# A graph kernel: low parts of the value items, taken from a ScalarE copy and subtracted later

## The chip, the cores and the metric

The kernel runs on one core of a Trainium2 chip. The metric is the device time of one execution in microseconds (us). PE is TensorE, DVE is VectorE, ACT is ScalarE, POOL is GpSimd, SP is SyncE; PEld is TensorE's loading of weights.

## The reference, cut to what matters

1024 nodes with 512 features, 16384 edges (src, dst) sorted by dst.

```
h = relu(layernorm(x));  q, k, v = h @ Wq + bq, h @ Wk + bk, h @ Wv + bv
adj[src, dst] = 1
a = where(adj, q @ k.T / sqrt(512), -1e6)
x = x + softmax(a) @ v
h = relu(layernorm(x))
deg = number of edges into a node + 1;  w = deg^-0.5[src] * deg^-0.5[dst]   # with self loops
agg(y) = segment_sum(w * y[dst], src)
x = x + agg(relu(batchnorm(agg(h @ W1 + b1))) @ W2 + b2)
```

What the change touches is `h @ Wv`, 1024x512, and `softmax(a) @ v`.

## The kernel before, in words

**Products in parts.** Most operands are held as two parts of TensorE's rounded format (fp32r): high = the rounded value, low = the value minus high. A product is three matmuls (lines 955 to 957): low x high, high x low, high x high. So every product that is used again is evacuated from PSUM twice: ScalarE writes the high part (hi_of, line 450), VectorE subtracts it from the same PSUM bank to give the low part (lo_of, line 645).

**Items.** A piece of such work is called an item: "t" (a transposed weight), "m" (Wq Wk^T), "h" (128 rows of h, transposed), "v" (128 rows of h @ Wv, eight of them), "q" (128 columns for 512 rows of the query side), "w" (a row for the mask level). `items` lists them in TensorE's order, and `nth(item)` is an item's place in it, counted from 1. The semaphores item_ps (TensorE done), item_hi (ScalarE done) and item_lo (VectorE done) count in this order. TensorE's make(item) (line 971) waits until the last item in the same PSUM bank has its low part (`last_in`, line 183), and an item that reads others waits for their low parts by item_lo.

**Counting stage.** The adjacency counts are made in 16 windows of 64 target nodes (window 0, 1, ... in the order of work). The edges of a window come in chunks of 128. For each block of two or three chunks VectorE writes one-hot matrices, src_oh (line 674) and dst_oh (line 676), into a ring of four slots; TensorE multiplies them (line 1021), and a last matmul closes the window (line 1035). VectorE may write a slot again when TensorE has used it. ScalarE evicts the counts (counts, line 446), two banks taking turns. In between, items are worked off: before window i TensorE and ScalarE take the items `ahead[i]`, and VectorE takes their low parts two windows later, before its one-hots of window i + 2:

```
for i in range(2, NW):
    for item in ahead[i - 2]:
        lo_of(item)
    ...
    onehots(i, now)
```

The value items are in `ahead[2]` (v0, v1), `ahead[3]`, `ahead[4]` (v2, v3, each with an h item) and `ahead[6]` to `ahead[9]` (v4 to v7); `ahead[5]` holds two h items, `ahead[10]` to `ahead[13]` the first four q items, `ahead[15]` the w item.

**After the counts.** VectorE computes the mask level, the degrees (line 759) and the low part of the item q(1, 0) (line 763). GpSimd computes deg^-0.5 and then adds the value bias to four tiles of x (add_bv, line 381). TensorE goes over eight row tiles: scores(t) (line 1068), with the q items of the second half between the first ones, then weighted_v(t) (line 1082), the product of the probabilities p with all value items, and later products. For a tile VectorE masks the scores (line 775) and takes the maximum, ScalarE takes exp and writes the high part of p in half precision, VectorE its low part (line 787), two DMAs transpose the parts, and ScalarE (line 515) and VectorE (line 797) bring them back into p's place for weighted_v. Behind the first masking VectorE also finds whether a count is too large (large_flag, line 765). The order on each engine is that of the code.

**Places.** `v` is [128, 8, 2, 512] in fp32r: per value item its high part, then its low part.

Of the kernel before, what the change touches and what calls it, by code (L numbers as in the profile page):

```python
# [17 lines left out]
P = 128  # L18
N = 1024
D = 512  # L20
# [36 lines left out]
def gnn_kernel(nc, x, src, dst, Wq, bq, Wk, bk, Wv, bv, W1, b1, gamma, beta, W2, b2, out):  # L57
# [14 lines left out]
    def hold(name, kib):  # L72
# [18 lines left out]
        [("pT_place2", [P, 2, 2, NT, P], F32R), ("w2_raw", [P, 2, KC, D], F32)],  # L91
        [("g32", [P, KC, N], F32)])
    hold("region_WT", 32)
    v, zT, edge_i, edge_f, chunk1, hit, reach = shared(
        [("v", [P, NT, 2, D], F32R)], [("zT", [P, 2, KC, N], F32R)],
        [("edge_i", [P, 2, P], I32), ("edge_f", [P, 2, P], F32), ("chunk1", [P, 2, NCH], F32),
         ("hit", [P, 2, NCH], F32), ("reach", [P, 2, NCH], F32)])
    hold("region_v", 32)
# [57 lines left out]
    dst_in src_in ext_ready ext_ps edge_f_ready ecol_ps ecol_ready drel_ready lim_ready lim_ps bounds_ready  # L156
    x_in0 x_in1 x_in2 x_in3 qk_bias_in bcol_in bias_in b1_in
    Wk_in0 Wk_in1 Wq_in0 Wq_in1 wB_in0 wB_in1 w2_in0 w2_in1 w_hi w_lo
    x_sums x_means x_squares ln_scale ln_coef h_ready item_ps item_hi item_lo uw_ready hw_second fill_ready
    onehots onehots_used c_done c16 loops_added adj_in0 adj_in1 adj_in2 adj_in3  # L160
    deg_ready degm_ready degm_ps flag_ready dinv_ready
    s_ps mask_set masked top_ready exp_done rinv_ready p16_hi p16_lo p16_hi_in p16_lo_in p_hi p_lo pv_ps xb_ready x1_ready
# [16 lines left out]
    final = {("q", 1, c): 4 + c for c in range(KC)}  # L179
    items = list(start) + sum(ahead, []) + list(final)  # L180
    nth = lambda item: items.index(item) + 1
    item_bank = lambda item: start.get(item, final.get(item, 2 + (items.index(item) - len(start)) % ITEM_BANKS))
    last_in = lambda b, end: max([n for n, other in enumerate(items[:end], 1) if item_bank(other) == b] + [0])

    drel = lambda i: (drel_first if i < NW // 2 else drel_second)[:, i % (NW // 2), :]
    row_of = lambda t: T[:, t // 2, t % 2 * D:(t % 2 + 1) * D] if t < KC else hrow[:, t - KC, :]
# [222 lines left out]
    def _(act):  # L409
# [40 lines left out]
        def hi_of(item):  # L450

            what, n, c = item
            act.wait_ge(S["item_ps"], nth(item))
            if what == "q":
                if item == ("q", 0, 0):
                    act.wait_ge(S["uw_ready"], 4)
                if item == ("q", 1, 0):
                    act.wait_ge(S["c_done"], NW)
                act.activation(item_dest(item, 0), item_ps(item), ACT.Identity,
                               bias=uw[:, 0, c:c + 1]).then_inc(S["item_hi"], 1)  # L460
            else:
                act.activation(item_dest(item, 0), item_ps(item), ACT.Copy).then_inc(S["item_hi"], 1)

        def mask_fill(t):

# [131 lines left out]
    def _(dve):  # L597
# [47 lines left out]
        def lo_of(item):  # L645

            what, n, c = item
            dve.wait_ge(S["item_hi"], nth(item))
            hi = item_dest(item, 0).bitcast(F32)
            if what == "w":  # L650
                times_w_row(range(KC)).then_inc(S["item_lo"], 1)
            elif what == "q":
                dve.scalar_tensor_tensor(out=item_dest(item, 1), in0=item_ps(item),
                                         scalar=uw[:, 0, c:c + 1], in1=hi, op0=ALU.add,
                                         op1=ALU.subtract).then_inc(S["item_lo"], 1)
            else:
                dve.tensor_tensor(item_dest(item, 1), item_ps(item), hi, ALU.subtract).then_inc(S["item_lo"], 1)

        made = dve.alloc_register("made")
        dve.reg_mov(made, 0)  # L660
# [49 lines left out]
        def mask_level(blocks):  # L710

            if blocks.start == 0:
                dve.wait_ge(S["uw_ready"], 4)
                dve.wait_ge(S["item_lo"], nth(("w", 0, 0)))
            else:
                dve.wait_ge(S["hw_second"], 1)
            step(dve.tensor_scalar(hw[:, 1, blocks], hw[:, 0, blocks], bqbk[:, 0:1], -1.0, ALU.add, ALU.mult))
            dve.tensor_scalar(fill[:, blocks], hw[:, 1, blocks], NEG / SCALE, None, ALU.add).then_inc(S["fill_ready"], 1)
# [42 lines left out]
        dve.tensor_reduce(degm[:, 0:1], deg[:, :], AX.X, ALU.max).then_inc(S["degm_ready"], 1)  # L761
        dve.sem_inc(S["deg_ready"], 1)
        lo_of(("q", 1, 0))

        def large_flag():
            dve.wait_ge(S["degm_ps"], 1)
# [76 lines left out]
        for i in range(NT + 3):  # L843
            if i >= NT:
                h1_tmp(i - 3)
                h1_lo(i - 3)
            if 2 <= i <= NT:
                p_lo(i - 1)
            if 2 <= i <= NT + 1:
                h16_lo(i - 2)  # L850
            if i == NT:
                count_parts(DVE_COUNTS[2:])
            if i < NT:
                mask_and_max(i)
                add_loops(i)
            if 3 <= i < NT:
                h1_tmp(i - 3)
            if 2 <= i <= NT + 1:
                h2T_lo(i - 2)
            if i == NT + 1:  # L860
                split_w(2, 0)
                split_w(2, 1)
            if 3 <= i < NT:
                h1_lo(i - 3)
            if i == 0:
                large_flag()
                p16_lo(0)
                lo_of(("q", 1, 1))
                split_w(1, 0)
            if i == 1:  # L870
                p_lo(0)
                p16_lo(1)
                lo_of(("q", 1, 2))
                lo_of(("q", 1, 3))
                split_w(1, 1)
                times_w_row((4, 5))
            if i == 2:
                times_w_row((6, 7)).then_inc(S["hw_second"], 1)
                mask_level(slice(KC, NT))
            if i == NT - 1:  # L880
                dve.wait_ge(S["loops_added"], NT)
                count_parts(DVE_COUNTS[:1])
            if 1 <= i <= NT:
                residual(i - 1)
            if 2 <= i < NT:
                p16_lo(i)
            if i == NT - 1:
                count_parts(DVE_COUNTS[1:2])
# [63 lines left out]
    def _(pe):  # L952
# [18 lines left out]
        def make(item):  # L971
            what, n, c = item
            i = nth(item)
            if last_in(item_bank(item), i - 1):
                pe.wait_ge(S["item_lo"], last_in(item_bank(item), i - 1))
            if what in "htw":
                if what == "h":
                    pe.wait_ge(S["h_ready"], n + 1)
                elif what == "t":
                    pe.wait_ge(S[f"{'Wk' if n == K else 'Wq'}_in{c // 2}"], 16)  # L980
                    if item_bank(item) == 3:
                        pe.wait_ge(S["ecol_ready"], 2)
                else:
                    pe.wait_ge(S["uw_ready"], 4)
                for k in range(KC):
                    at = slice(k * P, (k + 1) * P)
                    rows = (row_of(n)[:, at] if what == "h" else qk_raw[:, n, c, at] if what == "t" else
                            uw[:, 1, k:k + 1].to_broadcast([P, P]))
                    m = pe.transpose(bank(item_bank(item))[:, at], rows, ident[:, :])  # L989
                m.then_inc(S["item_ps"], 1)  # L990
                return
            if what == "m":
                pe.wait_ge(S["item_lo"], nth(("t", Q, n)))
            else:
                pe.wait_ge(S["item_lo"], nth(("h", n if what == "v" else 4 * n + 3, 0)))
            if item == ("v", 0, 0):
                pe.wait_ge(S["w_lo"], LOADS)
            if item == ("q", 1, 2):
                pe.wait_ge(S["flag_ready"], 1)
            for k in range(KC):  # L1000
                if what == "v":
                    m = three(bank(item_bank(item)), lambda a: hT[:, a, k, n * P:(n + 1) * P],
                              lambda a: wB[:, a, k, :], k == 0, k == KC - 1)
                elif what == "m":
                    m = three(bank(item_bank(item)), lambda a: WT[:, Q, a, k, n * P:(n + 1) * P],
                              lambda a: WT[:, K, a, k, :], k == 0, k == KC - 1)
                else:
                    m = three(bank(item_bank(item)), lambda a: M[:, a, k, c * P:(c + 1) * P],
                              lambda a: hT[:, a, k, n * HALF:(n + 1) * HALF], k == 0, k == KC - 1)
            m.then_inc(S["item_ps"], 1)  # L1010
# [57 lines left out]
        def scores(t):  # L1068
            if t == 0:
                pe.wait_ge(S["c16"], 2 * NW)  # L1070
                pe.wait_ge(S["item_lo"], nth(("q", 0, KC - 1)))
            if t == 4:
                pe.wait_ge(S["item_lo"], len(items))
            if t >= 2:
                pe.wait_ge(S["masked"], t - 1)
            for n in range(2):
# [5 lines left out]
        def weighted_v(t):  # L1082
            pe.wait_ge(S["p_hi"], t + 1)
            pe.wait_ge(S["p_lo"], t + 1)
            if t >= 1:
                pe.wait_ge(S["x1_ready"], t)
            for k in range(NT):
# [3 lines left out]
        def times_w1(t):  # L1091
            pe.wait_ge(S["h2T_hi"], t + 1)
            pe.wait_ge(S["h2T_lo"], t + 1)
            if t == 0:
                pe.wait_ge(S["w_lo"], 2 * LOADS)
                pe.wait_ge(S["item_lo"], len(items))
            if t >= 1:
                pe.wait_ge(S["h1_tmp"], t)
            for k in range(KC):
# [33 lines left out]
        for i in range(NT):  # L1133
            scores(i)
            if i == 0:
                pe.wait_ge(S["degm_ready"], 1)
                pe.wait_ge(S["item_lo"], last_in(6, nth(("q", 1, 0))))
                pe.transpose(bank(6)[:, 0:P], degm[:, 0:1].to_broadcast([P, P]), ident[:, :]).then_inc(S["degm_ps"], 1)
                make(("q", 1, 1))
            if i == 1:  # L1140
# [98 lines left out]
```

## Time and profile before

| | us |
|---|---|
| median of 3 runs | 309.43 (309.1 to 310.83) |
| the profiled execution | 309.07 |
| its span, first to last instruction | 307.2 |
| TensorE busy | 295.4 (96% of the span) |
| VectorE busy | 210.1 (68%) |
| ScalarE busy | 143.6 (47%) |
| GpSimd busy | 56.5 (18%) |

The profile is of one execution. Matmuls are pipelined and their ends are modelled, so a busy TensorE is not TensorE at its peak. The granted TensorE clock was 1.000 (of 2.4 GHz) over the whole span.

### The profile page before, as it was taken

The numbers are of one execution on the slowest core, as the hardware profiler recorded it, in microseconds if no ns is written. First come the engines' busy times: TensorE is split into PE (matmuls) and PEld (weight loads), VectorE is DVE, ScalarE is ACT, GpSimd is POOL, SyncE is SP. The second block draws the span as 40 slices with busy tenths as digits, with TensorE's granted clock in tenths as the row PEclk, the third lists the DMA queues.
The fourth block names the chain that finished last, engine by engine and source line by source line (L and its number), as shares of the span: only waits on it lengthen the run. The fifth ranks groups of instructions, "written<-read, shape, count | busy, mean of one in ns | idle before, by whom it ended". The sixth has DMA issues, their size and how long they took to land.

```text
span 307.2 us, 4787 instructions
## 1 busy us (share of the span) xinstructions
PE 295.4 (96%) x1339; PEld 227.5 (74%) x1345; DVE 210.1 (68%) x472; ACT 143.6 (47%) x245; POOL 56.5 (18%) x94
## 2 busy tenths in 40 slices
PE   8999879899999999999999999999999999999995
PEld 6778346466565788888888888887888888878884
DVE  3798999999998648766757484667344388276311
ACT  3999924444346726635454445537623035343000
POOL 5352450000000340032121411203010044100000
PEclk9999999999999999999999999999999999999999
DMA  7815040000600308544452825223102000000221
GB/s 265 298 45 164 7 133 0 1 0 3 200 5 3 69 2 210 98 102 75 100 120 53 154 51 104 51 54 68 34 19 51 1 2 0 0 2 0 109 99 68
DMA packets 42312, 21.66 MB, mean 71 GB/s; under 512 B 35761, under 2 KB 36017, under 8 KB 42289
## 3 DMA queue, kind: packets, MB, share of 16 engines
q1 hardware_dynamic: 41744, 20.33, 26.5%
q10 hardware_dynamic: 544, 1.05, 0.9%
q8 instruction: 12, 0.20, 0.3%
q14 instruction: 12, 0.09, 0.1%
HBM read 10.88 MB, written 2.10 MB: 42 GB/s over the span
## 4 chain that ended last, share of the span: by engine, by line
PE 81%; DVE 7%; issue 4%; DVEq 3%; DMA 2%; ACT 1%; SPq 0%; ACTq 0%
PE ps L955 19%; PE ps L957 18%; PE ps L956 18%; PE ps L1205 10%; PE ps L1128 8%; PE ps L1021 7%; DVE src_oh L674 3%; DMA qk_raw<-L_gnn_Wq_in 2%; DVE dst_oh L676 1%; DVEq L674 1%; PE ps L989 1%; DVE T L775 0%; DVEq L666 0%; DVE smx L779 0%; DVE p L787 0%
## 5 line engine op out<-in xcount | busy, mean ns | idle before, releaser
L674 DVE TENSOR_SCALAR src_oh<-iota,ecol 128x512 f16 x149 | 44.3, 349 | 4.5 <-issue 3.4
L1021 PE MATMUL ps<-src_oh,dst_oh 128*128 x143 | 36.5, 382 | 6.2 <-DVE dst_oh L676 5.0
L1021 PEld LDWEIGHTS ps<-src_oh,dst_oh 128*128 x149 | 14.4, 104 | 25.7 <-issue 16.6
L1128 PE MATMUL ps<-cnt,qh 128*128 128x512 f32 x128 | 30.1, 391 | 0.3 <-ACT cnt L544 0.3
L1205 PE MATMUL ps<-qh,cnt 128*128 128x512 f32 x128 | 29.3, 390 | 0.0
L446 ACT ACTIVATE cnt<-ps 64x512 int16<-64x512 f32 x32 | 18.9, 591 | 20.7 <-PE ps L1035 20.3
L1128 PEld LDWEIGHTS ps<-cnt,qh 128*128 128x128 f32 x128 | 23.9, 188 | 5.6 <-DVE qh L834 0.7
L1205 PEld LDWEIGHTS ps<-qh,cnt 128*128 128x128 f32 x128 | 24.0, 188 | 5.2 <-DVE vb L936 0.3
L957 PE MATMUL ps<-v,pT 128*128 128x512 f32 x64 | 25.0, 390 | 0.0
L955 PE MATMUL ps<-hT,qh 128*128 128x512 f32 x64 | 24.9, 390 | 0.0
L955 PE MATMUL ps<-v,pT 128*128 128x512 f32 x64 | 24.9, 389 | 0.0
L956 PE MATMUL ps<-v,pT 128*128 128x512 f32 x64 | 24.9, 389 | 0.0
L956 PE MATMUL ps<-hT,qh 128*128 128x512 f32 x64 | 24.9, 389 | 0.0
L957 PE MATMUL ps<-hT,qh 128*128 128x512 f32 x64 | 24.9, 389 | 0.0
L385 POOL TENSOR_SCALAR lnb<-bnag 128x1 f32<-128x1 f32 x8 | 8.2, 1027 | 81.9 <-DVE bnag L808 81.9
L948 DVE SCALAR_TENSOR_TENSOR xt<-ps,dinv,x 128x512 f32<-128x512 f32 x8 | 5.7, 748 | 17.1 <-PE ps L1205 17.1
L500 ACT ACTIVATE T<-T,smx 128x1024 f32<-128x1024 f32 x8 | 9.2, 1155 | 16.2 <-DVE smx L780 16.2
L797 DVE TENSOR_SCALAR pT<-p16T 128x1024 fp32r<-128x1024 f16 x8 | 5.5, 693 | 15.7 <-DMA p16T<-p 15.6
L775 DVE COPY_PREDICATED T<-adj,ps 128x1024 f32<-128x1024 int16 x8 | 10.6, 1323 | 8.2 <-PE ps L957 8.2
L469 ACT ACTIVATE T<-zerob,fill 128x1024 f32<-128x1024 bf16 x8 | 9.1, 1146 | 12.1 <-DVE p L787 12.1
L676 DVE TENSOR_TENSOR dst_oh<-iota_w,drel_first 128x384 f16 (+1 forms) x35 | 14.4, 411 | 0.0
L528 ACT ACTIVATE hnT<-h16T 128x512 fp32r<-128x512 f16 x8 | 5.1, 632 | 19.8 <-DMA h16T<-h 19.8
(179 smaller groups left out, 660.4 us busy)
## 6 DMA issues: line engine op xcount, KB each, us to landing
xt<-x_in SPq DMA_DIRECT2D x16, 256.0 KB, 3.3
out<-xt SPq DMA_DIRECT2D x8, 256.0 KB, 2.1
qk_raw<-L_gnn_Wk_in ACTq DMA_DIRECT2D x2, 512.0 KB, 4.7
qk_raw<-L_gnn_Wq_in SPq DMA_DIRECT2D x2, 512.0 KB, 6.5
wB_raw<-L_gnn_Wv_in SPq DMA_DIRECT2D x2, 512.0 KB, 8.5
wB_raw<-L_gnn_W_in SPq DMA_DIRECT2D x2, 512.0 KB, 3.8
w_raw<-L_gnn_W_in SPq DMA_DIRECT2D x2, 512.0 KB, 4.3
bias_row<-L_gnn_b_in SPq DMA_DIRECT2D x2, 256.0 KB, 3.7
```

The lines of the kernel that those rows point to most:

```text
L446: act.activation(cnt16[rows, a * KC:(a + 1) * KC, w // 2, :], ps[a * WIN:(a + 1) * WIN, i % 2, :].rearrange("p (s n) -> p s n", n=P), ACT. ...
L469: act.activation(T[:, t % 2, :], zerob[:, 0:1].to_broadcast([P, N]), ACT.Identity, bias=fill[:, t:t + 1]).then_inc(S["mask_set"], 1)
L500: act.activation(T[:, t % 2, :], T[:, t % 2, :], ACT.Exp, bias=smx[:, 1, t:t + 1], scale=SCALE, accum_out=smx[:, 2, t:t + 1]).then_inc(S[" ...
L674: dve.tensor_scalar(src_oh[:, bass.ds(slot, 1), j, :].rearrange("p a n -> p (a n)"), iota[:, :], ecol[:, bass.ds(c + j, 1)], None, ALU.is_ ...
L676: dve.tensor_tensor(dst_oh[:, bass.ds(slot, 1), :, 0:count].rearrange("p a n u -> p (a n) u"), iota_w[:, :, 0:count], drel(i)[:, bass.ds(c ...
L775: dve.copy_predicated(T[:, t % 2, :], adj[:, t % ADJ, :], ps[:, 2 * (t % 2):2 * (t % 2) + 2, :].rearrange("p a n -> p (a n)")).then_inc(S[ ...
L955: pe.matmul(out_, stat(1), mov(0), start=first, stop=False)
L956: pe.matmul(out_, stat(0), mov(1), start=False, stop=False)
L957: return pe.matmul(out_, stat(0), mov(0), start=False, stop=last)
L1021: m = pe.matmul(ps[:, i % 2, :], dst_oh[:, bass.ds(slot, 1), :, j].rearrange("p a n -> p (a n)"), src_oh[:, bass.ds(slot, 1), j, :].rearra ...
L1128: m = pe.matmul(bank(g), qh[:, d, a, c * P:(c + 1) * P], cnt[:, d, n * HALF:(n + 1) * HALF], start=(d == 0 and a == 1), stop=last)
L1205: m = pe.matmul(bank(t), cnt[:, d, t * P:(t + 1) * P], qh[:, d, a, :], start=(d == 0 and a == 1), stop=last)
```

## The change

ScalarE, behind the high part of a value item, copies the same PSUM bank once more, unrounded, into the place of the low part (`v_raw`, the same memory as `v`, read as fp32). VectorE's low part of a value item in the counting stage goes. Instead VectorE subtracts the high part from the copy, in place, for six items behind the low part of q(1, 0), and for two behind large_flag. The bank of a value item is free when ScalarE's copy is done (semaphore v_raw), no longer when VectorE's low part is. weighted_v(0) waits for all eight subtractions (semaphore v_lo). item_lo counts all items but the value items now, so its waits use `nth_lo`.

```diff
-    v, zT, edge_i, edge_f, chunk1, hit, reach = shared(
-        [("v", [P, NT, 2, D], F32R)], [("zT", [P, 2, KC, N], F32R)],
+    v, v_raw, zT, edge_i, edge_f, chunk1, hit, reach = shared(
+        [("v", [P, NT, 2, D], F32R)], [("v_raw", [P, NT, 2, D], F32)], [("zT", [P, 2, KC, N], F32R)],
...
+    split_items = [item for item in items if item[0] != "v"]
+    nth_lo = lambda item: split_items.index(item) + 1
-    last_in = lambda b, end: max([n for n, other in enumerate(items[:end], 1) if item_bank(other) == b] + [0])
+    def left_bank(b, end):
+        before = [other for other in items[:end] if item_bank(other) == b]
+        if not before:
+            return None
+        if before[-1][0] == "v":
+            return S["v_raw"], before[-1][1] + 1
+        return S["item_lo"], nth_lo(before[-1])
...
                 act.activation(item_dest(item, 0), item_ps(item), ACT.Copy).then_inc(S["item_hi"], 1)
+            if what == "v":
+                act.activation(v_raw[:, n, 1, :], item_ps(item), ACT.Copy).then_inc(S["v_raw"], 1)
...
         def lo_of(item):
             what, n, c = item
+            if what == "v":
+                return
             dve.wait_ge(S["item_hi"], nth(item))
...
+        def v_lo(blocks):
+            for n in blocks:
+                dve.wait_ge(S["item_hi"], nth(("v", n, 0)))
+                dve.wait_ge(S["v_raw"], n + 1)
+                dve.tensor_tensor(v[:, n, 1, :], v_raw[:, n, 1, :], v[:, n, 0, :].bitcast(F32),
+                                  ALU.subtract).then_inc(S["v_lo"], 1)
...
         lo_of(("q", 1, 0))
+        v_lo(range(0, 6))
...
                 large_flag()
+                v_lo(range(6, NT))
                 p16_lo(0)
...
         def make(item):
-            if last_in(item_bank(item), i - 1):
-                pe.wait_ge(S["item_lo"], last_in(item_bank(item), i - 1))
+            left = left_bank(item_bank(item), i - 1)
+            if left:
+                pe.wait_ge(*left)
...
         def weighted_v(t):
             pe.wait_ge(S["p_lo"], t + 1)
+            if t == 0:
+                pe.wait_ge(S["v_lo"], NT)
```

## Rows read from the trace of the kernel before

**Rows 1.** The page: busy us of each engine; the chain by engine.

```profile
PE 295.4 (96%) x1339; PEld 227.5 (74%) x1345; DVE 210.1 (68%) x472; ACT 143.6 (47%) x245; POOL 56.5 (18%) x94
...
PE 81%; DVE 7%; issue 4%; DVEq 3%; DMA 2%; ACT 1%; SPq 0%; ACTq 0%
```

**Rows 2.** Waits, 55 to 90 us: who waited for whom, total us, times, longest.

```profile
ACT cnt L446 <- PE ps L1035: 12.0, 8, 2.5
...
PE ps L1021 <- DVE dst_oh L676: 1.7, 5, 0.5
```

**Rows 3.** By line: operation, times, duration in ns (least/median/most), first and last start.

```profile
L657 DVE TENSOR_TENSOR v<-ps,v x8: 676/680/684, 48.6 to 83.4; 128x512 fp32r<-128x512 f32 x8
...
L642 DVE TENSOR_TENSOR wB<-wB_raw,wB x4: 1212/1214/1216, 20.1 to 126.9; 128x1024 fp32r<-128x1024 f32 x4
...
L462 ACT ACTIVATE v<-ps x8: 592/597/601, 35.4 to 78.2; 128x512 fp32r<-128x512 f32 x8
```

**Rows 4.** Timeline of TensorE, counting stage: start us, duration us, engine, line, operation.

```profile
46.58 3.18 PE L1021 MATMUL ps<-src_oh,dst_oh 128*128 x14
...
52.90 2.54 PE L1021 MATMUL ps<-src_oh,dst_oh 128*128 x11
55.27 0.18 PE L1035 MATMUL ps<-zerob 128*128 128x32 bf16 x1
55.30 1.07 PE L989 MATMUL ps<-ident,hrow 128*128 128x128 f32 x8
...
60.41 0.18 PE L1035 MATMUL ps<-zerob 128*128 128x32 bf16 x1
...
65.04 0.18 PE L1035 MATMUL ps<-zerob 128*128 128x32 bf16 x1
...
70.17 0.18 PE L1035 MATMUL ps<-zerob 128*128 128x32 bf16 x1
...
89.04 0.18 PE L1035 MATMUL ps<-zerob 128*128 128x32 bf16 x1
...
93.00 0.18 PE L1035 MATMUL ps<-zerob 128*128 128x32 bf16 x1
```

**Rows 5.** Timeline of VectorE, counting stage (in brackets: idle before, and what ended it).

```profile
47.42 0.88 DVE L674 TENSOR_SCALAR src_oh<-iota,ecol 128x512 f16 x3 [0.72 <-PE ps L1021]
...
48.55 1.28 DVE L657 TENSOR_TENSOR v<-ps,v 128x512 fp32r<-128x512 f32 x2
...
55.18 0.60 DVE L674 TENSOR_SCALAR src_oh<-iota,ecol 128x512 f16 x2
```

**Rows 6.** Timeline of VectorE behind the counts.

```profile
105.31 0.75 DVE L653 SCALAR_TENSOR_TENSOR qh<-ps,uw,qh 128x512 fp32r<-128x512 f32 x1 [0.72 <-ACT qh L459]
110.13 1.34 DVE L775 COPY_PREDICATED T<-adj,ps 128x1024 f32<-128x1024 int16 x1 [4.06 <-PE ps L957]
...
113.44 0.14 DVE L769 CAST flag<-degm 1x1 int32<-1x1 f32 x1
115.36 1.23 DVE L787 SCALAR_TENSOR_TENSOR p<-T,p 128x1024 f16<-128x1024 f32 x1 [1.78 <-ACT p L508]
...
118.44 1.31 DVE L775 COPY_PREDICATED T<-adj,ps 128x1024 f32<-128x1024 int16 x1
```

**Rows 7.** GpSimd: its additions in the timeline, and one line by durations.

```profile
106.19 5.03 POOL L381 TENSOR_TENSOR xt<-xt,bias_row 128x512 f32<-128x512 f32 x4
...
L385 POOL TENSOR_SCALAR lnb<-bnag x8: 190/1222/1226, 131.1 to 224.7; 128x1 f32<-128x1 f32 x8
```

**Rows 8.** VectorE's low part of p, by durations.

```profile
L787 DVE SCALAR_TENSOR_TENSOR p<-T,p x8: 1224/1224/1227, 115.4 to 210.9; 128x1024 f16<-128x1024 f32 x8
```

**Rows 9.** Timeline of ScalarE and TensorE, the first p and its product.

```profile
122.38 1.04 ACT L515 ACTIVATE pT<-p16T 128x1024 fp32r<-128x1024 f16 x1
...
123.58 0.39 PE L955 MATMUL ps<-v,pT 128*128 128x512 f32 x1
```

More of the change, by code:

```diff
@@ L158, in gnn_kernel @@
     Wk_in0 Wk_in1 Wq_in0 Wq_in1 wB_in0 wB_in1 w2_in0 w2_in1 w_hi w_lo
-    x_sums x_means x_squares ln_scale ln_coef h_ready item_ps item_hi item_lo uw_ready hw_second fill_ready
+    x_sums x_means x_squares ln_scale ln_coef h_ready item_ps item_hi item_lo v_raw v_lo uw_ready hw_second fill_ready
     onehots onehots_used c_done c16 loops_added adj_in0 adj_in1 adj_in2 adj_in3
@@ L713, in mask_level @@
                 dve.wait_ge(S["uw_ready"], 4)
-                dve.wait_ge(S["item_lo"], nth(("w", 0, 0)))
+                dve.wait_ge(S["item_lo"], nth_lo(("w", 0, 0)))
             else:
@@ L992, in make @@
             if what == "m":
-                pe.wait_ge(S["item_lo"], nth(("t", Q, n)))
+                pe.wait_ge(S["item_lo"], nth_lo(("t", Q, n)))
             else:
-                pe.wait_ge(S["item_lo"], nth(("h", n if what == "v" else 4 * n + 3, 0)))
+                pe.wait_ge(S["item_lo"], nth_lo(("h", n if what == "v" else 4 * n + 3, 0)))
             if item == ("v", 0, 0):
@@ L1070, in scores @@
                 pe.wait_ge(S["c16"], 2 * NW)
-                pe.wait_ge(S["item_lo"], nth(("q", 0, KC - 1)))
+                pe.wait_ge(S["item_lo"], nth_lo(("q", 0, KC - 1)))
             if t == 4:
-                pe.wait_ge(S["item_lo"], len(items))
+                pe.wait_ge(S["item_lo"], len(split_items))
             if t >= 2:
@@ L1095, in times_w1 @@
                 pe.wait_ge(S["w_lo"], 2 * LOADS)
-                pe.wait_ge(S["item_lo"], len(items))
+                pe.wait_ge(S["item_lo"], len(split_items))
             if t >= 1:
@@ L1136, in _ @@
                 pe.wait_ge(S["degm_ready"], 1)
-                pe.wait_ge(S["item_lo"], last_in(6, nth(("q", 1, 0))))
+                pe.wait_ge(*left_bank(6, nth(("q", 1, 0))))
                 pe.transpose(bank(6)[:, 0:P], degm[:, 0:1].to_broadcast([P, P]), ident[:, :]).then_inc(S["degm_ps"], 1)
```

## Prediction

> **What bounds the kernel now.** I read the page first: TensorE is busy for 295.4 of 307.2 us and makes 81% of the chain that ended last, VectorE 7% [rows 1]. The stage in which VectorE paces TensorE is the counting, 28 to 101 us: there it builds the one-hot blocks that TensorE multiplies. The waits of 55 to 90 us show TensorE held up by VectorE's dst_oh, five times and 1.7 us in all, and ScalarE waiting eight times, 1.5 us each on average, for a window's closing matmul [rows 2]. VectorE has no idle row there. The eight low parts that the change moves lie inside this stretch, 679 ns each [rows 3], two in a row taking 1.28 us [rows 5], so 0.61 us each in a row. The wait rows understate the loss, because matmul ends are drawn late; I measure it by the window instead, from closing matmul to closing matmul.
>
> Window 6 (one value item, 8 chunks) runs from 60.41 to 65.04: 4.63 us, with no wait for VectorE. Window 12 (one query item, 5 chunks) runs from 89.04 to 93.00: 3.96 us, also without one [rows 4]. These are what TensorE needs. The others between them take longer:
> - Window 5 (two transposed items, 11 chunks): 60.41 - 55.27 = 5.14 us. Its own work is the 8 transposes, 1.07 us less a drawn-out end of 0.14, and 11 chunks, which took 55.27 - 52.90 = 2.37 us in window 4: 3.30 us. Lost: 1.84.
> - Window 7 (as window 6): 70.17 - 65.04 = 5.13, lost 0.50.
> - Windows 8 to 11 (own work 4.63, 4.63, 3.96, 4.63 = 17.85): 89.04 - 70.17 = 18.87, lost 1.02.
> Together 3.36 us. Windows 2 and 15 lose time to VectorE too, but no value low part lies ahead of the first, and before the last VectorE is itself held back by TensorE through the ring of four one-hot slots.
>
> **Low parts out of the counting stage.** VectorE loses 8 x 0.61 = 4.9 us there. What TensorE gets of it is followed window by window. Ahead of window 5 three low parts go (1.8 us), but its first block needs the ring slot of window 4's first block. How long that takes shows in window 3: TensorE began its chunks at 46.58 and VectorE, waiting for a slot, went on at 47.42, 0.84 us later [rows 4, 5]. TensorE begins window 4's chunks at 52.90, so VectorE can begin window 5 at 53.74 and not at 55.18 [rows 5]: 1.44 us earlier, of 1.84 lost. Ahead of window 6 another low part goes: VectorE leads by 2.05. Window 7 returns its 0.50 (1.94 used, lead 2.05). Ahead of windows 8 to 11 one more goes each time, the lead grows faster than TensorE uses it, and the 1.02 comes back. Sum: 1.44 + 0.50 + 1.02 = 2.96 us. From window 12 on TensorE is the bound and everything behind it, products to the last output, moves forward together. Lower bound: only the waits that the profile names, 1.7 less the 0.40 that the ring keeps, 1.3. Upper bound: 3.36. I take 2.96, since the windows without a wait lie between those with one and repeat their work.
>
> **The copies on ScalarE.** Eight more of 597 ns, out of the bank that was just read [rows 3], about 0.5 us each behind another. In windows 2 to 4 and 6 to 9 they stand ahead of the window's count eviction, for which ScalarE waits 1.5 us on average [rows 2]. They fit, at nothing. Without that cover the count eviction would be 0.5 us late, which decides nothing either until the bank is wanted two windows on. In window 2 they also push four layer-norm rows by 1 us, which the transposes use some 8 us later. The banks are freed by ScalarE now, earlier than before.
>
> **The moved subtractions, first six.** Behind the low part of the first late query item (105.31 + 0.75) VectorE waits 4.06 us, until 110.13, for the first scores [rows 6]. Six subtractions of two SBUF operands: the nearest row is the weights' 128x1024 at 1.214 us [rows 3], half of which is 0.61. 6 x 0.61 = 3.7 us fit with 0.4 to spare. They cost nothing unless something stretches them.
>
> **The last two.** They follow the flag, which ends at 113.58, and VectorE is idle until 115.36, 1.78 us [rows 6]; 1.22 fit, 0.56 is left. Behind them are queued the low part of p, a query item, a weight split and, at 118.44, the second masking; ScalarE's p at 122.38 (+1.04 = 123.42) depends on that, and TensorE takes p up at 123.58 [rows 9]. So the slack of this chain is 0.16 us: any delay of the masking steps over that stops TensorE. The new wait of the product of p with the value items, for all eight subtractions, stands behind this and decides nothing.
>
> **GpSimd beside them.** Its four bias additions run from 106.19 for 5.03 us [rows 7], over the first six subtractions. What two such neighbours do shows later: GpSimd's one-column step takes 190 ns alone and 1222 to 1226 in most cases, just as long as VectorE's two-operand low part of p that begins beside it, which keeps 1224 to 1227 in all eight [rows 7, 8]. So GpSimd waits out VectorE's instruction, and VectorE isn't stretched. The first subtraction would start at about 105.99 (105.31 + 0.75, less the 0.07 by which records in a row overlap [rows 5]), before GpSimd's addition at 106.19, and the six follow each other without a gap. I take it that the additions get in only behind the sixth, at 109.7, and end at 114.8. Nobody needs them before 129 us. But they then lie beside the last two subtractions. Bounds: if VectorE is never held, 0; if one addition (5.03 / 4 = 1.26) is waited out there, 1.26 - 0.56 - 0.16 = 0.54. The nearest row says 0, but it has no case with GpSimd first; I take the middle, 0.3.
>
> The Trainium skill (SBUF — State Buffer, SBUF: two separate sides) says that VectorE's second pair of ports is GpSimd's too, as an exclusive lock: an instruction of VectorE with two SBUF inputs and one of GpSimd that reads SBUF do not run together, and the first to start holds it to its end. The one-column rows agree for VectorE first; no row of this case shows GpSimd first. The old subtraction read PSUM, the new one reads SBUF twice, so the rule speaks against the change. By it the time is 306.5 to 307.0 with VectorE first, and rival 2's up to 310.9 with GpSimd first.
>
> **Sum.** The profiled execution took 309.07 us, 1.87 more than its span. 309.07 - 2.96 + 0.3 = 306.4. The median of the three timed runs is 309.43, 0.36 above that execution, so I forecast 306.4 + 0.4 = 306.8.
>
> **Rivals.**
> 1. The windows don't close up: the loss is in handing over each block (TensorE's wait behind each dst_oh), not in VectorE's amount of work. For it: the profile names only 1.7 us of waits. Against: windows 6 and 12 have the same hand-overs and lose nothing. Then 1.3 comes back, less 0.3: 308.4.
> 2. GpSimd first. If its additions begin before the subtractions, or get between them, VectorE waits 1.26 each time. All four: 106.06 + 5.03 + 3.66 = 114.75, so the first masking is 4.62 us late, and after the slack TensorE stops for 4.46: 309.43 - 2.96 + 4.46 = 310.9. The more additions VectorE waits for, the later: one costs 1.26 less 0.4 to spare and 0.16 slack, 0.7 (307.2); two 1.96 (308.4); from the third on the change is a loss (309.7). For it: only 0.2 us separates the two starts. Against: VectorE's pace beside GpSimd was untouched in every row read.
> 3. No collision, and the ring gives window 5 back whole: 309.43 - 3.36 = 306.1.
>
> **How the numbers follow.** Forecast 0.66, rival 1 0.14, rival 2 0.15, rival 3 0.05. The range is from 305.7 (rival 3 less 0.4, as the runs shown lie 0.33 below their median at the lowest) to 308.8 (rival 1 and two waits of rival 2 with the same 0.4); it leaves out the worst of rival 2 and little else. A measurement of this kernel tells about 0.5%, 1.55 us, from no change. Faster by more: forecast and rival 3, 0.71. Within: rival 1 and the milder half of rival 2, 0.19. Slower: 0.10, three or four additions of rival 2, which reach that bound only just, and what I don't see.
>
> **What would show it.** Window 5 closing 1.4 us earlier (about 59.0) and window 11 at about 86.1; ScalarE with 16 value copies; VectorE idle in the counting stage at the ring for the first time in these windows; six subtractions of about 0.68 us right behind the query low part, ending before the first masking at about 107.2; GpSimd's first addition drawn out to some 5 us; the first product with the value items at 120.6 to 121.2. The prediction is wrong if window 11 closes after 87.5, or if the first or second masking moves against the scores by over half a us.

## The result, and the profile after

The changed kernel takes 313.6 us (median of 17 runs, 311.0 to 315.35), the kernel before in the same comparison 310.46: a ratio of 1.010, interval 1.008 to 1.012. It is about 3 us slower; 306.8 and faster was forecast. The 309.43 that the forecast started from was the median of the first three of these 17 runs of the kernel before.

The page of the changed kernel: busy us by engine, and the granted clock in 40 slices.

```profile
PE 297.3 (95%) x1339; PEld 229.1 (74%) x1345; DVE 215.5 (69%) x472; ACT 147.7 (47%) x253; POOL 58.2 (19%) x94
...
PEclk9999999999999999699999999999999999999999
```

VectorE has as many instructions as before and is busy 5.4 us longer; TensorE's clock, which was full in every slice before, drops in one. The counting stage did become shorter. The closings of windows 3, 5, 6, 11 and 15 (timeline of TensorE), which answer to [rows 4]:

```profile
49.61 0.18 PE L1059 MATMUL ps<-zerob 128*128 128x32 bf16 x1
...
59.97 0.18 PE L1059 MATMUL ps<-zerob 128*128 128x32 bf16 x1
...
64.64 0.18 PE L1059 MATMUL ps<-zerob 128*128 128x32 bf16 x1
...
87.13 0.18 PE L1059 MATMUL ps<-zerob 128*128 128x32 bf16 x1
...
99.59 0.18 PE L1059 MATMUL ps<-zerob 128*128 128x32 bf16 x1
```

Window 3 closes where it did (49.59 before), window 11 closes 1.91 us earlier and window 15 1.89 (101.48 before). The loss comes right behind. For comparison, from the kernel before: window 15's closing, and the product behind the first one with the value items.

```profile
101.48 0.18 PE L1035 MATMUL ps<-zerob 128*128 128x32 bf16 x1
...
129.02 0.39 PE L955 MATMUL ps<-hT,qh 128*128 128x512 f32 x1
```

VectorE behind the counts, answering to [rows 6], the last row being the low part of p:

```profile
103.42 0.75 DVE L667 SCALAR_TENSOR_TENSOR qh<-ps,uw,qh 128x512 fp32r<-128x512 f32 x1 [0.72 <-ACT qh L469]
104.09 8.08 DVE L677 TENSOR_TENSOR v<-v_raw,v 128x512 fp32r<-128x512 f32 x6
112.09 1.31 DVE L797 COPY_PREDICATED T<-adj,ps 128x1024 f32<-128x1024 int16 x1
...
115.45 1.29 DVE L677 TENSOR_TENSOR v<-v_raw,v 128x512 fp32r<-128x512 f32 x2
117.30 1.23 DVE L809 SCALAR_TENSOR_TENSOR p<-T,p 128x1024 f16<-128x1024 f32 x1 [0.56 <-ACT p L520]
```

The six subtractions take 8.08 us and not 3.7; the two later ones 1.29. Taken one by one, with GpSimd's first two bias additions beside them:

```profile
104.09 0.68 DVE L677 TENSOR_TENSOR v<-v_raw,v 128x512 fp32r<-128x512 f32 x1
...
104.69 1.78 DVE L677 TENSOR_TENSOR v<-v_raw,v 128x512 fp32r<-128x512 f32 x1
...
106.39 1.77 DVE L677 TENSOR_TENSOR v<-v_raw,v 128x512 fp32r<-128x512 f32 x1
...
104.29 1.63 POOL L391 TENSOR_TENSOR xt<-xt,bias_row 128x512 f32<-128x512 f32 x1
...
105.88 1.73 POOL L391 TENSOR_TENSOR xt<-xt,bias_row 128x512 f32<-128x512 f32 x1
```

The first subtraction, begun 0.2 us before the first addition, takes its 0.68; that addition takes 1.63 in place of 1.29; the next subtraction takes 1.78, as it waits for the addition, and so on every 1.70 us until the four additions are done. The two engines take turns, instruction by instruction. The first masking begins at 112.09, 3.85 us later than 110.13 less the 1.89 won. TensorE, first product with the value items (the next product follows at 133.47):

```profile
121.47 0.39 PE L980 MATMUL ps<-hT,M 128*128 128x512 f32 x1
125.33 0.80 PE L978 MATMUL ps<-v,pT 128*128 128x512 f32 x1 [3.48 <-ACT pT L527]
125.92 0.63 PE L979 MATMUL ps<-v,pT 128*128 128x512 f32 x1
...
130.62 0.48 PE L978 MATMUL ps<-v,pT 128*128 128x512 f32 x1
...
133.47 0.39 PE L978 MATMUL ps<-hT,qh 128*128 128x512 f32 x1
```

Stretches: us, TensorE busy (instructions), its weight loads, VectorE, ScalarE, GpSimd, granted clock, DMA share and GB/s:

```profile
122.00:124.00 2.00, 0.00 (x0) 0.00 (x0) 1.76 (x4) 0.91 (x1) 0.00 (x0) 0.99 0.99 346
124.00:130.00 6.00, 4.67 (x11) 3.71 (x12) 3.74 (x6) 4.52 (x7) 0.00 (x0) 0.50 0.77 148
130.00:132.00 2.00, 2.00 (x8) 1.59 (x8) 1.22 (x4) 0.00 (x0) 0.00 (x0) 0.80 0.05 9
```

TensorE stands still for 3.48 us, and behind that its granted clock is 0.50 (the level of 1.2 GHz) from 124 to past 130: a matmul steps on after 0.43 us in place of 0.23. The sum of the profiled execution: the end of the counting -1.89; from there to the product 125.33 - 99.59 = 25.74 in place of 22.10, +3.64; the product 133.47 - 125.33 = 8.14 in place of 129.02 - 123.58 = 5.44, +2.70. Together +4.45; the span went from 307.2 to 311.6. The median moved less, 3.1 us: the profiled execution of the kernel before took 309.07 us, 1.4 under its median, that of the changed kernel 313.5, 0.1 under. The low clock doesn't last equally long in all executions either: of the 17 runs eight have a mean clock of 0.989 and take 314.2 us on average, five have 0.998 and take 311.7.

### The profile page after: what moved, and what is told of

Same layout as the page of the kernel before. It is cut to its first block, busy times and chain, and to the rows that moved or that the text cites. A ratio compares the mean times of both kernels' runs of the same rounds, so it can differ in the third digit from the quotient of the medians.

```text
span 311.6 us, 4803 instructions
## 1 busy us (share of the span) xinstructions
PE 297.3 (95%) x1339; PEld 229.1 (74%) x1345; DVE 215.5 (69%) x472; ACT 147.7 (47%) x253; POOL 58.2 (19%) x94
## 4 chain that ended last, share of the span: by engine, by line
PE 77%; DVE 12%; issue 4%; ACT 3%; DVEq 2%; DMA 1%; ACTq 0%
PE ps L978 17%; PE ps L980 17%; PE ps L979 17%; PE ps L1231 9%; PE ps L1154 8%; PE ps L1045 8%; DVE v L677 2%; DVE src_oh L695 2%; DMA qk_raw<-L_gnn_Wk_in 1%; PE ps L1013 1%; DVE T L797 1%; DVE smx L801 1%; DVEq L695 1%; DVE dst_oh L697 1%; DVE WT L671 1%
## 5 line engine op out<-in xcount | busy, mean ns | idle before, releaser
L978 PE MATMUL ps<-v,pT 128*128 128x512 f32 x64 | 26.1, 408 | 3.5 <-ACT pT L527 3.5
L980 PE MATMUL ps<-v,pT 128*128 128x512 f32 x64 | 25.9, 405 | 0.0
L979 PE MATMUL ps<-v,pT 128*128 128x512 f32 x64 | 25.9, 404 | 0.0
L978 PEld LDWEIGHTS ps<-v,pT 128*128 128x128 f32 x64 | 12.7, 198 | 6.6 <-ACT pT L527 3.9
L979 PEld LDWEIGHTS ps<-v,pT 128*128 128x128 f32 x64 | 12.7, 198 | 2.7
L980 PEld LDWEIGHTS ps<-v,pT 128*128 128x128 f32 x64 | 12.6, 197 | 2.7
```

The costliest lines, as they stand in the source:

```text
L978: pe.matmul(out_, stat(1), mov(0), start=first, stop=False)
L979: pe.matmul(out_, stat(0), mov(1), start=False, stop=False)
L980: return pe.matmul(out_, stat(0), mov(0), start=False, stop=last)
```

## The experiments

Theory: VectorE's subtractions with two SBUF operands and GpSimd's additions take turns on a shared access to SBUF; the masking is late, TensorE stands still, and its clock falls. Rivals: the gap was too short for them anyway, or ScalarE's copies and the new waits are the cause. Executions differ by up to 1.45 us ahead of window 3's closing (49.6 to 51.0; 50.85 in experiment 2, whose kernel is the one before up to there), so positions below are counted from that closing. Each time is compared with the kernel before in the same session. The code is cut to what matters (...).

**1. One operand from PSUM.**
```
-  dve.tensor_tensor(v[:, n, 1, :], v_raw[:, n, 1, :], ...
+  from_bank = n < 6
+  if from_bank:
+      dve.wait_ge(S["v_raw"], NT)
+  dve.tensor_tensor(v[:, n, 1, :], bank(7) if from_bank else v_raw[:, n, 1, :], ...
```


> The changed kernel, but the first six subtractions read a PSUM bank (that of value item 7) and the high part, one SBUF input each in place of two; the low parts of the first six value items are therefore those of other data. Theory (VectorE instructions with two SBUF inputs and GpSimd's bias additions take turns): no subtraction over 0.75 us, the six take 3.7 us in place of 8.1, GpSimd's four additions 5.0 us in place of 6.7, the first masking at 108.2 +- 0.4, no stall of TensorE before the first product with the value items, granted clock 1.00, time 1.5 to 2.0 us under the kernel before. Rival (the place is too short, or the subtractions are held by something else than GpSimd): the six still take 8 us and the time stays about 3 us above the kernel before.

Measured: 307.77 us, ratio 0.9924 (0.990 to 0.9949), 2.1 us under the kernel before. Subtractions by line (durations least/median/most in ns) and GpSimd's additions:

```profile
L680 DVE TENSOR_TENSOR v<-ps,v x6: 683/683/683, 105.3 to 108.3; 128x512 fp32r<-128x512 f32 x6
...
105.57 5.07 POOL L391 TENSOR_TENSOR xt<-xt,bias_row 128x512 f32<-128x512 f32 x4
```

The same place, engine, length and neighbours, one SBUF input fewer: nothing is stretched, and the clock stays at 1.00. The theory holds; the place and the copies are not the cause.

**2. The suspect alone, in the kernel before.**
```
   lo_of(("q", 1, 0))
+  for n in range(6):
+      dve.wait_ge(S["item_lo"], nth(("v", n, 0)))
+      dve.tensor_tensor(v[:, n, 1, :], v[:, n, 1, :].bitcast(F32), v[:, n, 0, :].bitcast(F32), ALU.subtract)
```


> The kernel before with one thing added: six subtractions of two SBUF operands behind the low part of q(1, 0), over the low parts of value items 0 to 5 (which it spoils). Nothing is taken out of the counting stage and ScalarE copies nothing more. Theory: the six take about 8.1 us beside GpSimd's additions, the first masking comes about 4 us late (114), TensorE stalls some 3.7 us before the first product with the value items, the granted clock falls for some 5 us behind it, and the time is 5.5 to 6.5 us above the kernel before. Rival (the loss comes from ScalarE's copies or the new waits): six of 0.61 us, which fit in the 4.06 us gap; time as before.

Measured: 315.03 us, ratio 1.0153 (1.0122 to 1.0185), 5.1 us above the kernel before, a little under the range expected; the profiled span is 6.5 us longer, of which 1.3 lie ahead of window 3's closing.

```profile
107.26 8.08 DVE L766 TENSOR_TENSOR v<-v 128x512 fp32r<-128x512 f32 x6
...
107.47 6.72 POOL L381 TENSOR_TENSOR xt<-xt,bias_row 128x512 f32<-128x512 f32 x4
...
128.51 0.80 PE L958 MATMUL ps<-v,pT 128*128 128x512 f32 x1 [3.48 <-ACT pT L515]
...
135.45 0.39 PE L958 MATMUL ps<-hT,qh 128*128 128x512 f32 x1
...
130.00:132.00 2.00, 2.00 (x7) 1.60 (x6) 2.00 (x5) 1.70 (x2) 0.00 (x0) 0.65 0.69 132
```

The same 8.08 us, the same standstill, without any other part of the change. The granted clock falls to 0.50 here too, but it is back sooner (0.65 from 130 to 132, the last row): the product takes 135.45 - 128.51 = 6.94 us, 1.50 more than before and not 2.70. This fits a time a little under the range.

**3. A GpSimd instruction that reads nothing.**
```
-  pool.tensor_tensor(xt[:, n % XT, :], xt[:, n % XT, :], bias_row[:, 0, :], ALU.add)...
+  if t < XT:                                # the first four tiles
+      pool.iota(xt[:, n % XT, :], pattern=[[1, D]], ...
```


> The changed kernel, but GpSimd's first four bias additions are replaced by index patterns that it writes into the same tiles and that read nothing (x and the value bias are left out of the first four row tiles). Theory A (only a GpSimd instruction that reads SBUF takes turns with VectorE's two reads): the six subtractions take 3.7 us, time 1.5 to 2.0 us under the kernel before. Theory B (any GpSimd instruction on SBUF does): subtractions beside the patterns take about 0.6 us more each, up to 2.3 us in all, the first masking is up to 1.9 us late, TensorE stalls up to 1.7 us.

Measured: 308.33 us, ratio 0.9944 (0.9918 to 0.997).

```profile
105.54 3.69 DVE L681 TENSOR_TENSOR v<-v_raw,v 128x512 fp32r<-128x512 f32 x6
...
105.76 2.12 POOL L392 IOTA xt<- 128x512 f32 x4
```

Side by side for 2.1 us and no subtraction over 0.69: theory A. It is reading on both sides that collides; GpSimd's writing alone doesn't.

**4. The additions later.**
```
   if t == 0:
       pool.wait_ge(S["bias_in"], 16)
+      pool.wait_ge(S["w_lo"], LOADS + 1)
```


> The changed kernel, but GpSimd's first bias addition waits until the first split of the second weight is subtracted (line split_w(1, 0) on VectorE, about 118 us). Theory: the six subtractions take 3.7 us, the first masking comes at 108.2, TensorE doesn't stall, granted clock 1.00, and the additions, now beside the second masking and its maximum (one SBUF input each), delay VectorE by under 0.5 us: time 1.4 to 2.0 us under the kernel before. Rival (GpSimd isn't the cause): the six still take 8 us, time about 3 us above the kernel before.

Measured: 308.33 us, ratio 0.9953 (0.9933 to 0.9974), 1.6 us under the kernel before. The six take 3.69 us. What the additions touch now (timeline of VectorE, their start at 116.79):

```profile
119.37 1.32 DVE L650 TENSOR_TENSOR cnt<-cnt,identb 128x128 int16<-128x128 int16 x1
120.62 1.80 DVE L820 TENSOR_SCALAR pT<-p16T 128x1024 fp32r<-128x1024 f16 x1
...
122.52 0.47 PE L979 MATMUL ps<-v,pT 128*128 128x512 f32 x1 [0.55 <-issue]
```

The masking and its maximum pass beside them unharmed, but the add of the self loops, which has two SBUF inputs, takes 1.32 us in place of 0.22, and bringing back the low part of p, which has one SBUF input, 1.80 in place of 0.69. TensorE waits 0.55 us. I had not looked at these two.

**5. The additions earlier, in the counting stage.**
```
+  for t in range(XT):
+      add_bv(t)
   pool.wait_ge(S["deg_ready"], 1)
   pw(dinv[:, :], deg[:, :], NT)...
   ...
-  for t in range(XT):
-      add_bv(t)
```


> The changed kernel, but GpSimd makes its four bias additions ahead of the degree power, as soon as the value bias has landed (about 84 us, in the counting stage, where it was idle). Theory: the six subtractions take 3.7 us and the stall goes; the additions now take turns with dst_oh (two SBUF inputs) in windows 10 to 12, where VectorE has some 3 us of lead, so TensorE loses under 1 us there: time 0.8 to 2.0 us under the kernel before. Rival (the collision costs the same wherever it falls): VectorE loses about 4 us in the counting stage and TensorE 2 or more; time not under the kernel before.

Measured: 307.87 us, ratio 0.993 (0.9906 to 0.9953), 2.0 us under the kernel before. The additions are at 84.5 to 89.8, and there src_oh and dst_oh are stretched (one addition each):

```profile
84.07 1.92 DVE L695 TENSOR_SCALAR src_oh<-iota,ecol 128x512 f16 x3
85.91 1.51 DVE L697 TENSOR_TENSOR dst_oh<-iota_w,drel_second 128x384 f16 x1
```

But VectorE has lead there: window 11 closes 37.56 behind window 3, as without the additions (37.52), window 15 0.35 later. The collision costs where its victim has no slack. Run once more on another chip:

> The kernel e3_adds_early once more, for comparison on the same chip: 1.5 to 2.2 us under the kernel before, window 11 closing 37.4 to 37.7 us behind window 3.

Measured: 308.75 us, ratio 0.9971 (0.9954 to 0.9989), window 11 at 37.55; 0.6 us under the kernel before, less than expected, while the profiled execution, from window 3's closing on, is 1.6 us shorter, as in the first run (1.65). The gain of this version is between 0.3 and 0.7%; more exactly the two runs don't tell.

**6. The clock.**
```
   if i == 1:                                # ahead of weighted_v(0)
+      pe.wait_ge(S["item_lo"], nth_lo(("q", 1, 0)))
+      for _ in range(30):
+          pe.matmul(bank(4)[:, 0:P], zerob[:, :], zerob[:, :], start=True, stop=True)
```


> The changed kernel with 30 matmuls of zeros (128x128, some 0.11 us each) ahead of the first product with the value items, in the place where TensorE stood still for 3.5 us. Theory (the stall costs twice: TensorE stands still, and its granted clock then falls to 1.2 GHz for some 5 us): the product starts at the same time or up to 0.5 us later, but its matmuls take 0.39 us from the first on, the granted clock stays at 1.00, and the time is 2 to 3 us under the changed kernel's 313.6, that is 0.3 to 1.2 us above the kernel before. Rival (the clock falls for another reason, or its fall is made good later): time as the changed kernel, 1% above the kernel before.

Measured: 312.24 us, ratio 1.0077 (1.0052 to 1.0102): 2.4 us above the kernel before, where 0.3 to 1.2 were expected, and 1.4 under the changed kernel's median of another session, where 2 to 3 were. The interval overlaps with the changed kernel's (1.008 to 1.012), so the times alone don't show what the clock costs; the traces do.

```profile
122.72 1.85 PE L1172 MATMUL ps<-zerob 128*128 128x128 bf16 x30
126.36 0.50 PE L978 MATMUL ps<-v,pT 128*128 128x512 f32 x1 [1.79 <-ACT pT L527]
126.70 0.40 PE L979 MATMUL ps<-v,pT 128*128 128x512 f32 x1
...
131.97 0.39 PE L978 MATMUL ps<-hT,qh 128*128 128x512 f32 x1
...
126.00:128.00 2.00, 1.64 (x7) 1.36 (x8) 0.71 (x1) 2.00 (x4) 0.00 (x0) 1.00 0.32 66
```

The zeros filled half of the standstill, as one took 0.06 us and not 0.11; 1.79 us of standing still did not bring the clock down, 3.48 did. The product takes 131.97 - 126.36 = 5.61 us in place of 8.14. So the second part of the loss is the clock's: 2.5 us between these two executions. From window 3's closing to the end the filled one is 2.4 us shorter (310.2 - 50.60 = 259.6 against 311.6 - 49.61 = 262.0).

**7. The bounds load behind the first block.** On top of the early additions:
```
-  if i + 1 < NW:
-      bounds = bounds_of(i + 1)                 # ahead of the window
   ...
   chunks_of(i, first, LEAD)                     # its first block
+  following = ahead_of_loop() if ahead_of_loop else None     # bounds_of(i + 1)
```


> The kernel with the early additions (e3_adds_early), and in the counting stage VectorE's queue loads the next window's bounds (0.30 + 0.20 us) behind the window's first block and no longer ahead of it. It is about window 5, which came 0.44 us earlier where 1.44 were forecast. Theory (the value items' low parts had covered this load, so that removing them uncovered it): window 4's first block starts about 0.5 us earlier than 49.26, window 5 closes 0.4 to 0.9 us earlier against window 3's closing, and the time is 0.3 to 0.9 us under e3_adds_early's, 2.3 to 2.9 under the kernel before. Rival (the ring of four slots holds the first block back): nothing moves in window 5, time as e3_adds_early, 2.0 under the kernel before.

Measured: 309.15 us, ratio 0.9975 (0.9959 to 0.9992). Window 5 closes at 10.67 and window 11 at 37.93, 0.3 to 0.4 us later than in experiment 5 (10.36, 37.56), where 0.4 to 0.9 earlier was expected. Timeline of VectorE, window 4 (window 3 closes at 50.15), and the load in its queue (duration in ns, start):

```profile
49.17 0.62 DVE L695 TENSOR_SCALAR src_oh<-iota,ecol 128x512 f16 x2
49.70 0.42 DVE L697 TENSOR_TENSOR dst_oh<-iota_w,drel_first 128x256 f16 x1
50.68 0.88 DVE L695 TENSOR_SCALAR src_oh<-iota,ecol 128x512 f16 x3 [0.56 <-PE ps L1044]
...
L687 DVEq TENSOR_LOAD <-lohi x1: 303/303/303, 49.6 to 49.6; - x1
```

The first block did move, to 0.98 us ahead of the closing (0.35 in the changed kernel), so the ring does not hold it; the idle time went behind it (0.56). Between the load at 49.6 and the next one-hots at 50.68 the queue's records follow each other without a gap as long as 0.1 us. The queue's work is the limit wherever it stands, and behind one short block it is covered worse.

**8. Two low parts kept in the counting stage.** On top of the early additions, VectorE subtracts value items 0 and 1 from PSUM as before:
```
-  if what == "v":
+  if what == "v" and n >= KEPT:             # KEPT = 2
       return
   ...
-  v_lo(range(0, 6))
+  v_lo(range(KEPT, 6))
```


> The kernel with the early additions, and the low parts of value items 0 and 1 stay in the counting stage, subtracted from PSUM as in the kernel before; the other six go as in the change (four behind the low part of q(1, 0), two behind the flag). It is again about window 5. Theory (those two low parts only covered VectorE's queue while it loads bounds and computes addresses at a window's start, so taking them out freed next to nothing): window 5 closes 10.2 to 10.5 us behind window 3's closing, as in e3_adds_early (10.36; 10.82 in the kernel before), window 11 37.4 to 37.7 us behind it, and the time is that of e3_adds_early within 0.5 us. Rival (each low part costs TensorE its 0.61 us until the ring stops it): keeping two gives back most of window 5's 0.46 us, it closes at 10.7 or later, and window 11 0.4 us or more later than in e3_adds_early.

Measured: 307.99 us, ratio 0.9951 (0.9933 to 0.9969). Window 5 closes at 10.43, window 11 at 37.61, 0.07 and 0.05 us later than with all eight moved: the theory. Taking these two out had freed next to nothing. The time is 0.8 us under that of the early additions in the same session (308.75) where 0.5 at most was expected; the windows decide here, and not the times. A ring that holds the block would give the same closings; against it speaks experiment 7.

## Why the prediction was wrong

**The step that failed: "I take it that the additions get in only behind the sixth".** From rows with one VectorE instruction beside one of GpSimd [rows 7, 8] I concluded that VectorE keeps its pace and GpSimd waits. With several in a row on both sides they take turns: VectorE, having begun first, still waited for all four additions. Rival 2 named the case ("or get between them") and priced it at 1.26 us an addition, but had 0.15; it came with VectorE first, which I had held to be the safe case: 8.08 us in place of 3.7. The Trainium skill (SBUF — State Buffer, SBUF: two separate sides) describes an exclusive lock that the first to start holds for its whole instruction, and limits it, for two SBUF inputs, to GpSimd instructions that read SBUF. The rows agree instruction by instruction, each engine waiting until the other's instruction is done, and experiment 3 agrees with the limit. That section does not say who is next; the rows do.

**The slack** was right: the masking 3.85 us late, the product 3.64 late, for 0.16 of slack. So were the last two subtractions: they fit, and 0.56 us is left, as worked out.

**A term that was missing: the clock.** Rival 2 had TensorE's standstill and nothing after it: 310.9. The standstill brought the granted clock down to 0.50, and the product behind it cost 2.70 us more in the profiled execution. It is what makes the difference between a loss of 1.75 (3.64 - 1.89) and one of 4.45. Its size is not the same each time: in experiment 2 it was 1.50 behind the same standstill.

**The counting stage: 1.9 of 2.96.** Windows 6 to 11 gave back 28.63 - 27.16 = 1.47 us where 1.52 was forecast, though VectorE began window 6 only 0.92 us earlier (59.69, before 60.61) and not with the lead of 2.05 that was worked out: this part came true with half the lead it counted on, which is luck in part. Window 5, sized at 1.44, gave 0.46. Timeline of VectorE, and the load of the bounds and the address work in its queue (durations in ns, first and last start):

```profile
47.44 0.88 DVE L695 TENSOR_SCALAR src_oh<-iota,ecol 128x512 f16 x3 [0.68 <-PE ps L1045]
...
49.26 0.62 DVE L695 TENSOR_SCALAR src_oh<-iota,ecol 128x512 f16 x2 [0.61 <-PE ps L1045]
...
54.28 0.62 DVE L695 TENSOR_SCALAR src_oh<-iota,ecol 128x512 f16 x2
...
L687 DVEq TENSOR_LOAD <-lohi x1: 301/301/301, 48.2 to 48.2; - x1
L687 DVEq FUSED_REGOPS  x1: 204/204/204, 48.5 to 48.5; - x1
L695 DVEq FUSED_REGOPS  x2: 53/59/65, 49.0 to 49.2; - x2
```

The two low parts that stood at 48.55 to 49.75 [rows 5] lay over this load and the address work behind it. Without them window 4 begins at 49.26, 0.49 us earlier and not 1.2, and window 5 at 54.28 in place of the 53.74 that the ring would allow. The profile puts the 0.61 us down to TensorE, but the queue's records follow each other from the load at 48.2 to 49.2, the one-hots come right behind them, and experiment 7 shows that the ring was open. I had cost low parts at their duration without asking what they covered.

That accounts for most of window 5's later start. Of the 0.90 us by which VectorE still began it earlier than before (54.28, 55.18 before), half was lost inside the window. The last block's one-hots, before and after:

```profile
58.28 0.86 DVE L674 TENSOR_SCALAR src_oh<-iota,ecol 128x512 f16 x3
...
57.83 0.88 DVE L695 TENSOR_SCALAR src_oh<-iota,ecol 128x512 f16 x3
```

From the first block's start to the last's it is 3.55 us in place of 3.10, and TensorE closes the window that much less early. Why the blocks lie further apart no run takes apart; this part stays open.

**ScalarE's copies** cost nothing, as forecast: it still waits 7.7 us in eight times for closings between 55 and 90 us (12.0 before), and all gains of experiments 1, 3 and 5 are had with them.

## What to carry to other kernels

An operand that moves from PSUM to SBUF may make its instruction collide with a neighbour it never met: look at what GpSimd reads at that time, and price every one of its instructions in that stretch, whoever begins first. Where a chain has 0.2 us of slack before TensorE, price a standstill of some us twice, once for the wait and once for the clock behind it (3.48 us brought it down here; 0.55 and 1.79 us did not). And an instruction that is taken out frees only what it didn't cover.

## What the runs showed of the hardware

- VectorE with two SBUF inputs and GpSimd reading SBUF alternate, 1.70 us a pair here (alone 0.68 and 1.29; the records overlap); with one input from PSUM (683 ns in all six) or GpSimd only writing (no subtraction over 0.69 us) they don't notice each other.
- Instructions of VectorE with one SBUF input can be hit too: the half-precision return of p (1.80 in place of 0.69) and src_oh were, the masking and its maximum (1.34 and 1.22) were not.
- After 3.48 us of standstill TensorE's granted clock was at 0.50, in the changed kernel for over 6 us, in experiment 2 for less (0.65 from 130 to 132); after 1.79 us, behind 1.85 us of small matmuls, it stayed at 1.00.
- At a window's start VectorE's queue loads the bounds (0.30 us) and works on addresses (0.20 us and more behind it), and this shows as idle time where VectorE has nothing queued ahead of it: 0.61 us ahead of window 4.
